# Two graph layers on one core: a new opening from columns of x, and a last row with its own banks and its own output queue

## The reference

```
h = relu(layernorm(x));  x = x + gnn(h, adj)
h = relu(layernorm(x));  x = x + leaky(agnn(leaky(agnn(h))))

gnn:   h1 = tanh-map(atanh-map(h) @ embed)  (+) embed_bias
       n  = tanh-map(adj @ atanh-map(h1))
       out = tanh-map(atanh-map([h, n]) @ layer)  (+) layer_bias
agnn:  softmax(where(adj > 0, beta * (xn @ xn.T), -1e9)) @ x,   xn = rows of x over their length
```

## Time and profile before

| what | value |
|---|---|
| median of 3 runs | 976.91 us (976.67 to 977.71) |
| the profiled execution, its own time | 978.14 us |
| its span, first to last instruction | 976.6 us |
| mean granted clock of PE | 0.989 |
| busy: PE / DVE / ACT / POOL | 929.2 / 818.8 / 511.2 / 8.0 us |
| product with `adj` begins | 57.41 us |
| last store issued | 972.90 us |

### The profile page before, as it was taken

One profiled execution on the slowest core, in us unless ns is written; L12 is line 12 of the kernel. 1 busy time (PEld: TensorE's weight loads), 2 busy tenths in 40 slices (PEclk: granted clock), 3 DMA queues, 4 the chain that ended last, 5 costly groups with the idle time before them and its releaser, 6 DMA issues.

```text
span 976.6 us, 22955 instructions
## 1 busy us (share of the span) xinstructions
PE 929.2 (95%) x9012; PEld 695.3 (71%) x9012; DVE 818.8 (84%) x2110; ACT 511.2 (52%) x756; POOL 8.0 (1%) x21
## 2 busy tenths in 40 slices
PE   2989999999996999999999999999999999999996
PEld 2944444444444878888888888778888888888885
DVE  7891888888889987888989898998778887888887
ACT  1711122212126685766656667787565565656564
POOL 0000000000000000000000000000000000000000
PEclk9899999999998999999999999999999999999999
DMA  8338988888861445565465555545565655665630
GB/s 301 143 118 285 307 285 287 277 295 283 301 229 44 174 173 207 196 246 212 179 235 192 222 217 193 180 167 217 197 217 198 246 197 204 221 232 189 246 142 36
DMA packets 29971, 207.26 MB, mean 212 GB/s; under 512 B 3632, under 2 KB 4272, under 8 KB 5296
## 3 DMA queue, kind: packets, MB, share of 16 engines
q1 hardware_dynamic: 28224, 203.44, 57.6%
q0 software_dynamic: 640, 2.10, 0.5%
q10 hardware_dynamic: 1008, 0.33, 0.1%
HBM read 203.75 MB, written 2.10 MB: 211 GB/s over the span
## 4 chain that ended last, share of the span: by engine, by line
PE 69%; DVE 22%; issue 5%; ACT 3%; DMA 1%; DVEq 0%; POOL 0%; SPq 0%; POOLq 0%
PE s_ps L622 17%; PE s_ps L608 10%; PE acc_ps L469 6%; PE acc_ps L675 6%; PE acc_ps L671 6%; PE acc_ps L673 6%; PE acc_ps L652 5%; PE acc_ps L648 5%; PE acc_ps L650 5%; DVE small L1132 1%; DVE small L1134 1%; DVE small L1133 1%; DVE work L1647 1%; ACT work L990 1%; PE s_ps L427 1%
## 5 line engine op out<-in xcount | busy, mean ns | idle before, releaser
L990 ACT ACTIVATE work<-s_ps,beta_bias,beta_scale 128x1024 f32<-128x1024 f32 x144 | 173.4, 1204 | 217.0 <-PE s_ps L622 216.9
L469 PE MATMUL acc_ps<-ring,set 128*128 128x512 f32 x512 | 223.8, 596 | 3.2 <-DVE set L1245 3.2
L1665 DVE SCALAR_TENSOR_TENSOR h_all<-ring,s_ps 128x1024 f32<-128x1024 f32 x112 | 136.7, 1221 | 65.5 <-PE s_ps L608 64.3
L469 PEld LDWEIGHTS acc_ps<-ring,set 128*128 128x128 f32 x512 | 96.8, 191 | 120.3 <-issue 117.6
L1647 DVE TENSOR_TENSOR work<-work 128x1024 f16<-128x1024 f32 x96 | 132.5, 1380 | 5.4 <-ACT work L1000 5.4
L1000 ACT ACTIVATE work<-work 128x1024 f16<-128x1024 f32 x96 | 131.5, 1369 | 3.2 <-DVE work L1655 0.2
L1655 DVE SCALAR_TENSOR_TENSOR work<-ring,work 128x1024 f32<-128x1024 f32 x96 | 116.8, 1217 | 0.0
L622 PE MATMUL s_ps<-xt 128*128 128x512 f16 x432 | 106.4, 382 | 3.8 <-ACT work L990 3.0
L622 PE MATMUL s_ps<-set 128*128 128x512 f16 x432 | 105.0, 379 | 0.5 <-ACT work L990 0.5
L671 PE MATMUL acc_ps<-set,work 128*128 128x129 f16 x576 | 102.4, 219 | 2.7 <-DVE accs L1682 2.7
L671 PE MATMUL acc_ps<-src,work 128*128 128x129 f16 x576 | 103.5, 220 | 1.4 <-DVE work L1655 1.4
(11 more groups left out here) (260 smaller groups left out, 1723.2 us busy)
## 6 DMA issues: line engine op xcount, KB each, us to landing
ring<-in_adj_t SPq DMA_DIRECT2D x192, 1024.0 KB, 5.0
x_sb<-in_x SPq DMA_DIRECT2D x4, 512.0 KB, 7.2
out<-x_sb POOLq DMA_DIRECT2D x8, 256.0 KB, 2.8
w<-in_layer ACTq DMA_DIRECT2D x2, 64.0 KB, 8.1
w<-in_embed ACTq DMA_DIRECT2D x1, 64.0 KB, 4.2
eb<-in_embed_bias ACTq DMA_DIRECT2D x1, 64.0 KB, 6.9
lb<-in_layer_bias ACTq DMA_DIRECT2D x1, 64.0 KB, 7.9
beta<-in_beta ACTq DMA_DIRECT2D x2, 0.5 KB, 7.2
```

Source lines behind the costliest of these rows:

```text
L469: last = nc.tensor.matmul(agg, v_sb[:, jb, :], ring[:, k, b, :], start=jb == 0, stop=jb == NB - 1)
L990: nc.scalar.activation(values[x.n % VR], score_ps, ACT.Exp, bias=beta_bias[:, x.la:x.la + 1], scale=beta_scale[:, x.la:x.la + 1]).then_inc ...
L1665: V.scalar_tensor_tensor(turned[x.off % MR].rearrange("p (b j) -> p b j", b=CB), ring[:, x.mir_tile % AR, :, ds(x.h * HB * P, HB * P)], 0. ...
```

## The change

It has two parts that share nothing.

**The opening.** A second copy of the input, `x_t` (x transposed, made on the host), is loaded in four pieces between those of `x`, a piece of `x_t` first. PE no longer waits for DVE's statistics: it multiplies a matrix `centre` (identity minus 1/128, made by DVE) by 512 columns of `x_t` at once (`h_columns`), which subtracts the mean of each row of x. ACT applies ReLU (`h_out`) and squares the result into `sq_sb` (`h_squares`); PE sums the squares of a block with a product by a column of ones (`h_lengths`). The division by the deviation is left out of the rows and put into the numbers: DVE multiplies the squared lengths and one factor by the inverse deviation or its square, and ACT scales `h1` by it, four instructions a chunk in the place of one. `web` becomes column 129 of `w1`, so that one product gives `g` and `gb` together (`products`), and the separate one-column products are gone. The squared lengths no longer cost DVE its 32 instructions, nor the normed rows their 32. `products` of chunks 0 to 3 stand between the columns, one for every two chunks, those of 4 to 7 behind. Three of the `h1_out` stand ahead of the Tanh. Four products for warmth stand at the very start and thirty, in the place of ten, ahead of the product with `adj`; these wait for `closing`, which DVE raises behind `product_scalars`.

**The end.** Row 15 is summed in banks of its own (`last_own_ps`, in `s_ps`) and its totals go to memory of their own (`sums_last`), so its first half doesn't wait for row 14's total. DVE's order is written out: the mask of half 143 comes ahead of row 14's total and of the last flush. Row 15 is finished by DVE alone (`last_row`: leaky step on the sums, then one instruction a block that scales and adds). Its chunk is stored by SP, the other seven by POOL.

```diff
-    WARM = 10
+    WARM = 30
+    EARLY_WARM = 4
...
+        sums_last = src0_all[:, 0:2 * CB * PW].bitcast(f32).rearrange("p (b w) -> p b w", w=PW)
...
-        g_ps = [s_ps[:, i, 0:CH].rearrange("p (b f) -> p b f", f=F) for i in range(2)]
+        g_ps = [s_ps[:, i, :].rearrange("p (k n) -> p k n", k=2)[:, :, 0:2 * PW] for i in range(2)]
...
+        hh_ps = acc_ps[:, 0, 0:NB]
...
+        ht_ps = [acc_ps[:, 1 + i, :] for i in range(3)]
...
+        last_own_ps = g_ps[1]
...
+            def x_columns(i):
+                sp.dma_start(xt_in_sb[:, ts(i, N // XP)], x_t[:, ts(i, N // XP)]).then_inc(xt_in[i], 16)
+
+            def x_rows(i):
+                sp.dma_start(x_sb[:, ts(i, NB // XP), :], x_v[:, ts(i, NB // XP), :]).then_inc(x_in[i], 16)
+
+            x_columns(0)
             for i in range(XP):
-                sp.dma_start(x_sb[:, ts(i, NB // XP), :], x_v[:, ts(i, NB // XP), :]).then_inc(x_in[i], 16)
+                if i + 1 < XP:
+                    x_columns(i + 1)
+                x_rows(i)
...
+            sp.wait_ge(out_ready, NC)
+            sp.dma_start(out_v[:, ds((NC - 1) * CB, CB), :], x_sb[:, ds((NC - 1) * CB, CB), :])\
+                .then_inc(last_stored, 16)
+            sp.wait_ge(last_stored, 16)
...
-            with pool.Fori(0, NC) as c:
+            with pool.Fori(0, NC - 1) as c:
                 pool.wait_ge(out_ready, c + 1)
                 pool.dma_start(out_v[:, ds(c * CB, CB), :], x_sb[:, ds(c * CB, CB), :]).then_inc(stored, 16)
-            pool.wait_ge(stored, 16 * NC)
+            pool.wait_ge(stored, 16 * (NC - 1))
...
-            pe.wait_ge(embed_in, 16 * 2)
-
-
-            def h_transposes(r):
-                pe.wait_ge(xs_ready, r + 1)
-                wait(pe, ht_copied, r - 1)
-                for b in range(CB):
-                    last = nc.tensor.transpose(ht_ps[r % 2][:, ts(b, P)], scr_b[:, r * CB + b, :], ident[:, :])
-                last.then_inc(ht_done, 1)
-
-            h_transposes(0)
+            for _ in range(EARLY_WARM):
+                nc.tensor.matmul(acc_ps[:, 3, 0:P], ident[:, :], ident[:, :], start=True, stop=True)
+            pe.wait_ge(centre_made, 1)
+
+            def h_columns(r):
+
+                if r % 2 == 0:
+                    pe.wait_ge(xt_in[r // 2], 16)
+                wait(pe, ht_copied, r - 2)
+                nc.tensor.matmul(ht_ps[r % 3], centre, xt_in_sb[:, ts(r, CH)], start=True, stop=True)\
+                    .then_inc(ht_done, 1)
+
+            def h_lengths(r):
+
+                pe.wait_ge(ht_squared, r + 1)
+                for b in blocks(r):
+                    last = nc.tensor.matmul(hh_ps[:, b:b + 1], sq_sb[:, ts(b, P)], ones[:, 0:1], start=True, stop=True)
+                last.then_inc(hh_done, 1)
+
+            def products(r):
+                wait(pe, g_copied, r - 1)
+                for b in range(CB):
+                    last = nc.tensor.matmul(g_ps[r % 2][:, b // 2, ts(b % 2, PW)], ht_sb[:, ts(r * CB + b, P)],
+                                            w1[:, 0:PW], start=True, stop=True)
+                last.then_inc(g_done, 1)
+
+            h_columns(0)
+            h_columns(1)
             for r in range(NC):
-                if r + 1 < NC:
-                    h_transposes(r + 1)
-                pe.wait_ge(ht_copied, r + 1)
-                wait(pe, g_copied, r - 1)
-                for b in range(CB):
-                    last = nc.tensor.matmul(g_ps[r % 2][:, b, :], ht_sb[:, ts(r * CB + b, P)], w1[:, 0:F],
-                                            start=True, stop=True)
-                last.then_inc(g_done, 1)
-                if r == 0:
+                if r + 2 < NC:
+                    h_columns(r + 2)
+                h_lengths(r)
+                if r == 1:
                     pe.wait_ge(web_made, 1)
-                for b in blocks(r):
-                    last = nc.tensor.matmul(gb_ps[:, b:b + 1], ht_sb[:, ts(b, P)], web[:, :], start=True, stop=True)
-                last.then_inc(gb_done, 1)
+                if r % 2:
+                    products(r // 2)
+            for r in range(NC // 2, NC):
+                products(r)
...
+            pe.wait_ge(closing, 1)
             for _ in range(WARM):
...
+            def own_of(i):
+                return last_own_ps if i == LAST_ROW else own_ps
+
             def own_sum(x):
 
                 r = rows_of[x.row]
                 pe.wait_ge(own_made, x.n + 1)
                 if x.n == LAYER:
                     pe.wait_ge(consts_made, 9)
-                if x.n == r.first:
+                if x.n == r.first and x.row != LAST_ROW:
                     wait(pe, total_made, x.row)
+                own_ps = own_of(x.row)
...
+                    act.wait_ge(deviations_made, 1)
+                for b in range(CB):
+                    q = r * CB + b
+                    last = nc.scalar.activation(h1_sb[:, q, :], h1_ps[r % 4][:, b, :], ACT.Copy, scale=ext[:, q:q + 1])
+                last.then_inc(h1_copied, 1)
...
+            def h_out(r):
+                act.wait_ge(ht_done, r + 1)
+                nc.scalar.activation(ht_sb[:, ds(r * CH, CH)], ht_ps[r % 3], ACT.Relu).then_inc(ht_copied, 1)
+
+            def h_squares(r):
+                act.wait_ge(ht_copied, r + 1)
+                nc.scalar.activation(sq_sb[:, ds(r * CH, CH)], ht_sb[:, ds(r * CH, CH)], ACT.Square)\
+                    .then_inc(ht_squared, 1)
+
+            h_out(0)
             for r in range(NC):
-                act.wait_ge(ht_done, r + 1)
-                nc.scalar.activation(ht_sb[:, ds(r * CH, CH)], ht_ps[r % 2], ACT.Relu).then_inc(ht_copied, 1)
-                if r:
-                    g_out(r - 1)
+                if r + 1 < NC:
+                    h_out(r + 1)
+                h_squares(r)
+                if r % 2:
+                    g_out(r // 2)
+            for r in range(NC // 2, NC - 1):
+                g_out(r)
             log_terms(sm(4, NB), sm(5, NB), sm(6, NB))
             g_out(NC - 1)
+            for r in range(0, 3):
+                h1_out(r)
             on(ACT.Tanh, sm(5, NB), sm(4, NB))
-            for r in range(NC // 2):
+            for r in range(3, NC - 1):
                 h1_out(r)
             log_terms(sm(4, NB), sm(5, NB), sm(6, NB))
-            for r in range(NC // 2, NC):
-                h1_out(r)
+            h1_out(NC - 1)
...
+            dve.wait_ge(consts_made, 6)
+            V.tensor_scalar(centre, ident[:, :], -1.0 / F, None, ALU.add).then_inc(centre_made, 1)
...
-            inv_sqrt(sm(1, NB), sm(0, NB), sm(2, NB))
-            for r in range(NC):
-                for b in blocks(r):
-                    ins = V.tensor_scalar(scr_b[:, b, :], x_sb[:, b, :], mean_var[:, b, 0:1], small[:, 1, b:b + 1],
-                                          ALU.subtract, ALU.mult)
-                ins.then_inc(xs_ready, 1)
-            dve.wait_ge(xs_ready, NC)
...
-            for b in range(NB):
-                ins = V.scalar_tensor_tensor(v_sb[:, b, :], scr_b[:, b, :], 0.0, scr_b[:, b, :],
-                                             ALU.max, ALU.mult, accum_out=hh[:, b:b + 1])
-            step(ins)
+            step(V.tensor_scalar(sm(0, NB), mean_var[:, :, 1], LN_EPS, None, ALU.add))
+            inv_sqrt(ext[:, :], sm(0, NB), sm(2, NB))
+            step(V.tensor_tensor(sm(3, NB), ext[:, :], ext[:, :], ALU.mult))
+            dve.wait_ge(hh_done, NC)
+            ins = V.tensor_tensor(hh[:, :], hh_ps, sm(3, NB), ALU.mult)
+            ins.then_inc(deviations_made, 1)
+            dve.wait_ge(deviations_made, 1)
 
             norm(sm(0, NB), sm(1, NB), hh[:, :], EPS, NB)
             atanh_over(sm(2, NB), sm(0, NB), sm(1, NB), NB)
+            step(V.tensor_tensor(sm(2, NB), sm(2, NB), ext[:, :], ALU.mult))
             dve.wait_ge(g_copied, NC)
             norm(sm(0, NB), sm(1, NB), sm(10, NB), EPS, NB)
-            dve.wait_ge(gb_done, NC)
-            product_scalars(sm(0, NB), sm(2, NB), gb_ps, sm(10, NB), y2[:, 0:1], NB)
+            product_scalars(sm(0, NB), sm(2, NB), gb_sb, sm(10, NB), y2[:, 0:1], NB)
 
             xy, x2, rr, cross = (sm(i, NB) for i in (12, 13, 3, 9))
-            V.tensor_tensor(rr, xy, xy, ALU.mult)
-            V.tensor_tensor(cross, xy, gb_ps, ALU.mult)
+            V.tensor_tensor(rr, xy, xy, ALU.mult).then_inc(closing, 1)
+            V.tensor_tensor(cross, xy, gb_sb, ALU.mult)
...
-                both = sums_in.rearrange("p (k b) w -> p k (b w)", k=2)
+                sums = sums_last if i == LAST_ROW else sums_in
+                both = sums.rearrange("p (k b) w -> p k (b w)", k=2)
                 if r.a:
                     dve.wait_ge(row_summed, i + 1)
                     dve.wait_ge(flushed, half[r.first].la * NP + r.a * NC - r.a * (r.a + 1) // 2)
-                    V.tensor_tensor(both, own_ps, mirror_sums[:, ds(r.a * CB, CB), :]
+                    V.tensor_tensor(both, last_own_ps if i == LAST_ROW else own_ps, mirror_sums[:, ds(r.a * CB, CB), :]
```

(22 more changed lines are left out.)

52 lines of the change are left out of this document (30 added, 22 removed).

## The result

| | median, us | runs | ratio to before (95%) |
|---|---|---|---|
| before | 977.84 (976.67 to 980.9) | 6 | |
| the change | 985.88 (982.71 to 987.17) | 6 | 1.0072 [1.0049, 1.0096] |

The change is slower: by 7 us going by the ratio, by 8.0 us between the two medians. (The kernel before has three more runs here than in its own table, which moved its median from 976.91 to 977.84.) The profiled execution of the change took 982.71 us, the lowest of the six, with a span of 981.1 and a mean granted clock of 0.982. I forecast 980.8 within 971 to 986, and gave slower a chance of 0.56.

What follows compares the result with a forecast made beforehand. PE's groups cost most, but the change touches only the two ends, where engines wait in turn. Start +7.1, warmth −1.7 and end −1.5 make +3.9: 980.8 us from the median of 976.91, range 971 to 986.

Steps and rivals of the forecast that it cites:

- The serial cycle: Opening: PE and ACT wait for each other, 6.3 us for two chunks, 9.55 at half clock, against 4.35 before.
- the wait for Tanh: Opening, behind `norm`: three `h1_out` ahead of the table load make a wait of 1.6 us, up to 3.7 at half clock.
- my signs: Product with `adj` starting at 62 to 67, fourth `g_out` at 35 to 40, Tanh wait of 1.5 to 3.7 us.
- The start: Start of PE's product with `adj`: 64.5 us, 7.1 later than before.
- The middle of two ends: Opening: clock falls and returns in parts, so 64.5 was taken between starts of 58.0 (full clock) and 71 (half clock).
- the full-clock end: Opening at full clock after the first three columns: `norm` at 40.6, product with `adj` starting at 58.0.
- the third rival: Opening: half clock throughout, +13.6 − 3.2, 987 us; chance 0.08.
- Warmth: Ahead of the product with `adj`: thirty hidden products keep its first 4 us at full clock; gain 1.7, bounds 0 and 1.7.
- The end: Last row and store: last add 0.9 us sooner, SP's store saves 0.6 (bounds 0 and 1); together −1.5.
- Covers: Opening: DVE ready at 23 and the 64 instructions it loses are hidden; last piece of `x` at 17.
- Full clock: Opening, first rival: full clock through the cycles, +0.6 − 1.7 − 1.5, 974.3 us, faster; chance 0.23.
- Better overlap: Opening, second rival: ACT alone sets the pace, product with `adj` starts at 50 to 53, 968 us; chance 0.09.

Runs made afterwards that it cites:

- the repetition: The change itself, unedited, measured again on the same chip as three experiments: 986.43 us, ratio 1.0072.
- filled kernel: The change with products that nothing reads put into PE's pauses of the column stage and ahead of `h1`: 976.11 us, ratio 0.9985 to before.
- two others of the same opening: The kernel before with the new end, once with ten products for warmth (977.26 us), once with thirty (975.28 us).
- the last experiment: The change with PE and ACT in rounds, Tanh's table loaded early, and forty unread products ahead of `h1`: 969.92 us, ratio 0.9911 to before.
- the table early: The change with PE and ACT in rounds, and Tanh's table loaded directly behind the last `g_out`: 969.36 us, ratio 0.9900 to before.

## Why the prediction was right, and where it was off

*Direction and mechanism*: right. The serial cycle, the wait for Tanh and the mixed clock are all there, at the places named. The number is right by little: 985.88 is 0.12 us inside the range, the measured step between the medians (+8.0) is twice the +3.9 that I forecast, and the median of the repetition, 986.43, lies outside. Some of that is luck, and so is that the profiled execution met my signs: in the repetition's profile the fourth `g_out` (42.15, not 35 to 40) and the start (69.45, not 62 to 67) miss them.

*The start, forecast 64.5, +7.1.* Measured 65.73, +8.32. The 1.2 are two terms. The Tanh wait, which the two sums held at 1.6 and 3, middle 2.3, was 3.13: in the first 4 us of `h1`'s products the clock was low (0.61 on average from 48 to 52). And `norm`, which I put at 40.6 or 52, middle 46.3, started at 46.74.

*The middle of two ends* was a choice and not a mechanism, and the profile of the change can't say why the clock fell. The filled kernel says as much as is known: with unread work in PE's pauses the clock held in the profiled execution, and the full-clock end was right to 0.6 us (58.0 forecast, 58.60 measured). But taking the middle also made the low clock look like an even share of the time; from 28 to 40 it was low throughout, and in the repetition from 20 on (0.50 in both windows from 20 to 36), with the start at 69.45, outside my 62 to 67.

*The rule of the Trainium skill* (TensorE: Matmul & The Clock Gate, Part 1) says that an idle stretch takes the clock back. That it would leave the clock up through short pauses was my reading of it, and the trace of the change goes against that reading: the level was low in the execution whose pauses were 1.02 and 1.05 us at the first cycles, and 2.73 only later. That filling them kept it up agrees with the rule's core, that activity holds it.

*"8 us of pauseless work did not lift the clock before 27.2"*, my reason for the third rival, is what one execution did. In two others of the same opening it rose by 24 and by 33.

*Warmth, forecast 1.7.* Measured 1.70 in the product stage. Thirty products end 1.94 us before the long product starts, inside my 1.5 to 2.

*The end, forecast −1.5 (0.9 and 0.6).* Measured −2.16: 0.97 for the adds, 1.19 for the store. The store's term was mis-sized against this execution: I took 0.6 between bounds 0 and 1, and it lies above both; over the eleven executions with the new end it was 0.6 to 1.4. SyncE issued 0.02 us behind the last add where GpSimd took 0.72, and from the issue to the span's end were 3.21 us instead of 3.7. The 0.4 us that the Trainium skill (DMA: Bandwidth & Descriptors, Latency and other measured facts) would give for the path beside the wake-up is near the 0.49 of this execution; in the others it varies, down to nothing (3.78 us from the issue at 965.12 to the end in the last experiment).

*Covers.* DVE ready at 23: measured 24.1, and hidden by 12.5 us. Of the 64 instructions that it loses, some 15 us, I wrote that they are hidden; 2 to 3 us are not. Last `x` at 17: the last statistics waited until 16.10.

*The sum*: +3.9 against +4.5 between the profiled executions (982.71 less 978.14 is 4.57). What the prediction lacked is the spread: the median of the change lies 3 us above its profiled execution, and that alone brought the number to the edge of the range. The start of the kernel before spreads too (56.00 to 59.65), which I had taken as fixed at 57.41.

*The sign to look for, "last store issued by 971.5"*, was written in the time of the kernel before and left out that everything is shifted; taken back by the 6.66 us of the shift it is 971.23.

*The rivals.* Full clock (974.3) had 0.23 and is what the filled kernel realizes (975.57 profiled). Better overlap (start 50 to 53, 968) needed another order of both engines, as I wrote against it; with that order the start was 54.44, and 51.42 with the table early (969.36 us in the median, near that rival's 968).
